# LN1 statistics by sums and squares on ScalarE, and one of GpSimd's eight heads of tile 2 on VectorE

## The chip, the cores and the metric

The kernel runs on one core of a Trainium2 chip. The metric is the device time of that core in microseconds (us), the median of three runs. The engines are called as the profile calls them: PE is TensorE (matmuls), DVE is VectorE, ACT is ScalarE, POOL is GpSimd, SP is SyncE, which only issues DMAs.

## What is computed

8192 tokens of 256 numbers each go through an attention block, an MLP and a mixture of experts, all in fp32:

```python
def _layernorm(x, axis=-1, eps=1e-05):
    return (x - x.mean(axis)) / jnp.sqrt(x.var(axis) + eps)

x = x + _L0_attn_ref(_layernorm(x), ...)     # attention over 16 heads of one token, then an MLP with gelu
x = x + _L0_ffn_ref(_layernorm(x), ...)      # 8 experts, the two best of each token, and a shared expert

def _L0_attn_ref(q_x, ...):
    xn = _ln(q_x, ln1_w, ln1_b)              # a second normalisation, on the normalised input
    q, k, v = xn @ wq + bq, xn @ wk + bk, xn @ wv + bv      # 16 heads of 16
    fq, fk = elu(q) + 1, elu(k) + 1
    kv = einsum('bhnd,bhne->bnde', fk, v)    # sums over the heads of one token
    attn = einsum('bhnd,bnde->bhne', fq, kv) / (fq . sum_h fk + 1e-06)
    x = q_x + attn @ wo + bo
    return x + gelu(_ln(x, ln2_w, ln2_b) @ fc_w + fc_b) @ proj_w + proj_b
```

Two normalisations follow each other at the input: the outer one and LN1. Both need only the mean and the variance of a token's 256 inputs, so that they are done as one scale and one shift per token. With a variance v of the input, the product of the two factors is the root of 1/((v + eps)) times 1/(v(1 + eps) + eps*eps), up to a factor that cancels; the kernel computes both roots as exp(-0.5 ln(.)).

## The kernel before

**Blocks and stages.** The tokens are cut into 16 blocks of 512, a block into four tiles of 128 tokens, one token in each partition. The first phase, some 24 of the page's 40 slices, runs a loop over blocks, in which four stages of successive blocks overlap: in the body for block c the engines do the attention core of block c, the output projection, LN2 and the MLP of block c-1 (`stage_b`), routing and the first half of the shared expert of block c-2 (`stage_c`), and the second half of it for block c-3 (`stage_d`). The second phase gathers the tokens by expert and runs 71 expert tiles. The change touches the first phase alone.

**Who does what in a block.** PE transposes and projects each tile (`project_x`, L1256), runs the output projection (L1326), the shared expert's second half (`down`, L1420), the MLP's two layers (L1343, L1369) and the shared expert's first half (`shared_up`, L1404). The sums over heads of one token's attention are no matmuls: they are elementwise products and sums on DVE and POOL. The tiles are taken in the order 3, 0, 1, 2 (`ORDER`, L62), and their place in it, u = 0 to 3, is what the code calls a tile's number from here on. POOL does the place u = 0 whole. DVE does u = 1 and u = 3 whole. The place u = 2 (`SPLIT`) is divided: `POOL_HEADS` heads of it are POOL's, the rest DVE's (`own_heads`, L878).

**POOL's order in a block** (`body`, L553): the score products of u = 0 (L502), their sums by halving (L488, L498), the shared expert's gate product (L551), the mixing products (L509) and their sums, then `heads` (L520): the same four steps for its heads of u = 2, and last the eight indirect DMAs of `scatter` (L542). `scores` of u = 0 waits for DVE's features of that place (`feat_ready`, made at L869 near the end of DVE's body of the block before), and `heads` waits for DVE's features of u = 2 (L864).

**DVE's order in a block** (`body`, L1036): for u = 1 features, products (L884) and half of the sums (L893); then `residual_1` (L941), which waits for PE's output projection (L947), adds it and takes LN2's statistics; `keep_scales` (L855); `ln1_stats` for the next block (L830); `scales_b` (L848), which waits for ACT's reciprocal root of LN2 (`ln2_std`); the other half of the sums, the mixing products (L907); `ln1_scales` (L842), which waits for ACT's root of LN1; `choose` (routing); the sums (L920); then the same for u = 2 with DVE's heads of it, with `place` and `weights` (L1023 to L1028) in between; then u = 3 whole, with `residual_2`; and last the features of the next block's u = 0 (L869).

**LN1 statistics.** DVE takes them by `bn_stats` of each tile (L820) and `bn_aggr` (L827), which leaves mean and variance in `mv_a`, a piece of a PSUM bank. Two small operations add the epsilons (L836, L837). ACT takes logarithm and exponential (`rsqrt`, L665), DVE multiplies the mean by the factors (L842: one input in PSUM, `mv_a`, the other in SBUF, `rs_a`), and ACT applies the result to `xin` later (`norm_1`, L647).

**ACT's order around the change** (`body`, L695): after the projection of u = 2 has come from PE (`take_qkv`), the root of LN2 (`rsqrt`, sq_b and rs_b), LN2's normalisation of four tiles (L644, into a piece of `hid`), then the root of LN1 (sq_a and rs_a, L722), then the two copies of the transposed LN2 output (L726, `bT`). PE's first MLP layer (L1350) waits for these copies (`hT_ready`), and ACT's gelu follows it chunk by chunk.

Every engine takes its instructions in the order in which they are written. Waits are semaphores; a wait holds everything behind it on its engine.

Of the kernel before, what the change touches and what calls it, by code (L numbers as in the profile page):

```python
# [24 lines left out]
BF16 = mybir.dt.bfloat16  # L25
# [33 lines left out]
SPLIT = 2  # L59
POOL_HEADS = 8  # L60
RANKS_AT = 5
# [5 lines left out]
def build(nc, x, wqkv, b_tok, ln1w, ln1b, ln2w, ln2b, wo, fc_w, fc_b, proj_w, gate_w, sg_up, sg_down,  # L67
          experts, out):
    ctx = ExitStack()
    with ctx:  # L70
        def sb(name, shape, dt=FP32):
            return ctx.enter_context(nc.sbuf_tensor(name, shape, dt))

        def sem(name):
            return ctx.enter_context(nc.semaphore(name))
# [58 lines left out]
        rs_c = sb("rs_c", [P, 2, TPB])  # L134
        eps_1 = sb("eps_1", [P, 1])
        neg_1 = sb("neg_1", [P, 1])
        act_tmp = sb("act_tmp", [P, 4])
# [54 lines left out]
        def small(j):  # L192
            used = [D]

            def piece(n):
                used[0] += n
                assert used[0] <= 2 * D
                return p_qk[j][:, used[0] - n:used[0]]
            return (piece(2 * TPB).rearrange("p (t s) -> p t s", s=2),
                    piece(2 * TPB).rearrange("p (t s) -> p t s", s=2),  # L200
                    piece(3 * HEADS))
        mv_a, mv_b, _ = small(1)
        den = [small(j)[2] for j in range(2)]
# [19 lines left out]
        bias_ready = sem("bias_ready")  # L223
        xin_loaded = sem("xin_loaded")
        ln1_var = sem("ln1_var")
        ln1_log = sem("ln1_log")
# [73 lines left out]
        def wait(eng, s, value):  # L300

            if not isinstance(value, int) or value > 0:
                eng.wait_ge(s, value)
# [305 lines left out]
        def _(act):  # L609
# [31 lines left out]
            def norm(dst, src, scales, ready):  # L641

                for t in range(TPB):
                    a.activation(dst(t), src(t), ACT.Identity, bias=scales[:, 1, t:t + 1],  # L644
                                 scale=scales[:, 0, t:t + 1]).then_inc(ready, 1)

            def norm_1(b):  # L647
                wait(act, ln1_scale, b + 1)
                norm(lambda t: xin[:, t, :], lambda t: xin[:, t, :], rs_a[:, 1:4:2], xhat_ready)
# [45 lines left out]
            def body(c, j):  # L695
# [24 lines left out]
                if more:  # L720
                    wait(act, ln1_var, c + 2)
                    rsqrt(rs_a[:, 0:2], sq_a[:], ln1_log, ln1_std, c + 2)  # L722
                if stage_b:
# [36 lines left out]
            table_exp_ln()  # L760
            wait(act, ln1_var, 1)
            rsqrt(rs_a[:, 0:2], sq_a[:], ln1_log, ln1_std, 1)
            norm_1(0)
# [50 lines left out]
        def _(dve):  # L814
# [14 lines left out]

            def ln1_stats(b):  # L830

                wait(dve, xin_loaded, 16 * (b + 1))
                stats(lambda t: xin[:, t, :], mv_a)
                done.later(v.tensor_scalar(sq_a[:, 0, :], mv_a[:, :, 1], 1.0, EPS, ALU.mult, ALU.add))  # L836
                v.tensor_scalar(sq_a[:, 1, :], mv_a[:, :, 1], 1.0 + EPS, EPS * EPS,  # L837
                                              ALU.mult, ALU.add).then_inc(ln1_var, 1)

            def ln1_scales(b):  # L840
                wait(dve, ln1_std, b + 1)
                v.scalar_tensor_tensor(rs_a[:, 2:4], mv_a[:, :, 0].unsqueeze(1).to_broadcast([P, 2, TPB]), -1.0,  # L842
                                       rs_a[:, 0:2], ALU.mult, ALU.mult).then_inc(ln1_scale, 1)
# [192 lines left out]
            def body(c, j):  # L1036
# [10 lines left out]
                if core:  # L1047
                    keep_scales(c)
                    if more:
                        ln1_stats(c + 1)  # L1050
                if stage_b:
# [87 lines left out]

            dve.wait_ge(pool_const, 4)  # L1140
            ln1_stats(0)
            done(v.memset(neg_1[:], -1.0))
            done(v.memset(eps_1[:], EPS))
            announce(dve, v.memset(act_tmp[:], 0.0), tmp_ready, 1)
            ln1_scales(0)


# [416 lines left out]
```

## Time and profile before

| | us |
|---|---|
| median of three runs (lowest, highest) | 1806.62 (1806.27, 1808.12) |
| the profiled execution's own time | 1806.18 |
| its span, from the first to the last instruction | 1804.5 |

| engine | busy us | share of the span |
|---|---|---|
| PE matmuls | 1700.4 | 94% |
| POOL | 1244.4 | 69% |
| DVE | 1214.8 | 67% |
| ACT | 723.5 | 40% |

The shares are averages over two very different phases. In the page's forty slices DVE and POOL stand at eight or nine tenths in the first 24 slices, which is the block loop, and at two or three tenths after that; PE stands at nine tenths in both. The mean granted PE clock of the whole span is 0.971. The chain that ended last, followed back through the whole span, is 43% PE, 41% POOL, 7% DVE and 7% issue.

How to read it: a row of the timeline begins with the start and the duration in us, then the engine, the line, the operation, what it writes and reads, and in brackets the idle time of the engine before it and what ended that. "x4" is four instructions of one kind in a row. Rows of grouped lines end with the busy time in us, the mean duration of one instruction in ns, and the idle time before.

### The profile page before, as it was taken

Reading aid. Unit: us, or ns where it says so; the run is one execution under the profiler, and the core shown is the slowest. Engines: PE = TensorE matmul, PEld = TensorE weight load, DVE = VectorE, ACT = ScalarE, POOL = GpSimd, SP = SyncE. Lnnn points to the kernel's source line nnn. Section 1 sums busy time; section 2 is a strip of 40 time slices with the busy share of each in tenths; the row PEclk is TensorE's granted clock in tenths of the full one; section 3 lists DMA queues with packets and bytes.
Section 4 is the critical chain, followed back from the end, with each engine's and each line's share of the span. In section 5 each row is a group of like instructions: output and inputs, shape, how many; then the busy total and the mean of one; then the engine's idle time right before and its main releaser. Section 6 shows DMA issues by size and latency. Waiting matters only on the chain.

```text
span 1804.5 us, 25211 instructions
## 1 busy us (share of the span) xinstructions
PE 1700.4 (94%) x7288; PEld 1236.1 (69%) x7289; DVE 1214.8 (67%) x2292; ACT 723.5 (40%) x1469; POOL 1244.4 (69%) x652
## 2 busy tenths in 40 slices
PE   2588999999999999999999998989999999999997
PEld 1354675665666666666666666658888888888886
DVE  7999999999999999999999986132222222222221
ACT  2244445445455355355354363322323232323232
POOL 5988899999999899898899994223333333333333
PEclk8688999999999999999999999989999999999999
DMA  5101101101101101101101101156777677777774
GB/s 199 43 4 59 48 21 39 60 15 44 56 15 47 47 23 47 47 23 47 47 23 47 47 13 36 36 155 162 167 154 169 151 167 155 168 152 165 156 167 78
DMA packets 87150, 148.79 MB, mean 82 GB/s; under 512 B 8640, under 2 KB 71872, under 8 KB 86720
## 3 DMA queue, kind: packets, MB, share of 16 engines
q1 hardware_dynamic: 60512, 112.58, 20.0%
q0 software_dynamic: 26592, 35.67, 12.0%
q8 instruction: 20, 0.33, 0.1%
q14 instruction: 26, 0.21, 0.0%
HBM read 101.79 MB, written 48.56 MB: 83 GB/s over the span
## 4 chain that ended last, share of the span: by engine, by line
PE 43%; POOL 41%; issue 7%; DVE 7%; DMA 1%; ACT 1%; POOLq 1%; SPq 0%; DVEq 0%; ACTq 0%
POOL prod_pool L488 16%; PE p_b L1473 10%; PE p_b L1484 10%; POOL prod_pool L509 8%; POOL prod_pool L502 7%; PE p_q L1473 7%; POOL rows_sorted L542 5%; PE p_b L1301 4%; PE p_v L1473 3%; PE p_b L1350 2%; POOL sg_g L551 2%; PE p_xT L1460 2%; PE p_b L1416 2%; DVE p_q L893 1%; DVE prod L884 1%
## 5 line engine op out<-in xcount | busy, mean ns | idle before, releaser
L596 POOL DMA_INDIRECT out_rows<-prod_pool,prod x142 | 220.7, 1554 | 384.1 <-ACT prod_pool L790 353.7
L488 POOL TENSOR_TENSOR prod_pool<-prod_pool 128x2048 f32<-128x2048 f32 (+2 forms) x192 | 400.9, 2088 | 15.1
L1350 PE MATMUL p_b<-bT,fc_sb 128*128 128x512 f32 x512 | 230.7, 605 | 1.3 <-ACT bT L726 1.3
L1301 PE MATMUL p_b<-proj_sb,hid 128*128 128x256 f32 x1024 | 231.6, 379 | 0.0
L1301 PEld LDWEIGHTS p_b<-proj_sb,hid 128*128 128x128 f32 x1024 | 189.8, 190 | 29.2 <-issue 0.5
L1473 PE MATMUL p_b<-prod,exp_up 128*128 128x256 f32 x840 | 187.1, 379 | 0.0
L1416 PE MATMUL p_b<-x3T,sgup_sb 128*128 128x512 f32 x384 | 177.3, 601 | 5.4 <-DVEq L968 3.5
L884 DVE TENSOR_TENSOR prod<-p_q,eqk 128x4096 f32<-128x4096 f32 (+1 forms) x48 | 178.3, 3714 | 4.8
L893 DVE TENSOR_REDUCE p_q<-prod 128x128 f32<-128x2048 f32 x64 | 180.7, 2823 | 1.2
L907 DVE TENSOR_TENSOR prod<-p_q,v_dve 128x4096 f32<-128x4096 f32 (+1 forms) x48 | 178.2, 3713 | 1.7
L920 DVE TENSOR_REDUCE qkv<-prod 128x256 f32<-128x4096 f32 (+1 forms) x48 | 178.0, 3709 | 1.7
L1350 PEld LDWEIGHTS p_b<-bT,fc_sb 128*128 128x128 f32 x512 | 97.6, 193 | 113.2 <-issue 106.0
L1473 PEld LDWEIGHTS p_b<-prod,exp_up 128*128 128x128 f32 x840 | 157.0, 190 | 19.8
L1235 DVE TENSOR_TENSOR prod_pool<-prod,p_b 128x256 f32<-128x256 f32 x105 | 44.2, 421 | 180.9 <-ACT prod L782 130.4
L542 POOL DMA_INDIRECT rows_sorted<-rows,slot x128 | 127.0, 992 | 51.0 <-issue 37.5
L1273 PE MATMUL p_q<-wqkv_sb,xnT 128*128 128x512 f32 x256 | 128.3, 625 | 33.0 <-DVEq L939 21.4
L502 POOL TENSOR_TENSOR prod_pool<-fqk_pool 128x4096 f32<-128x4096 f32 x16 | 121.0, 7562 | 31.4 <-DVE fqk_pool L869 30.7
L731 ACT ACTIVATE hid<-p_b,fcb_sb 128x512 f32<-128x512 f32 x128 | 87.9, 687 | 128.4 <-PE p_b L1350 128.4
L1473 PE MATMUL p_q<-prod,exp_up 128*128 128x256 f32 x576 | 132.7, 384 | 0.0
L1416 PEld LDWEIGHTS p_b<-x3T,sgup_sb 128*128 128x128 f32 x384 | 69.1, 192 | 86.4 <-issue 65.2
L629 ACT ACTIVATE eqk<-p_q,neg 128x512 f32<-128x512 f32 x64 | 44.0, 687 | 209.4 <-PE p_v L1278 160.3
L790 ACT ACTIVATE prod_pool<-p_b,prod 128x256 f32<-128x256 f32 x142 | 59.5, 470 | 160.5 <-PE p_b L1484 156.0
(175 smaller groups left out, 2965.4 us busy)
## 6 DMA issues: line engine op xcount, KB each, us to landing
exp_up<-in_experts SPq DMA_DIRECT2D x71, 768.0 KB
prod<-rows_sorted SPq DMA_DIRECT2D x71, 260.0 KB
xin<-in_x SPq DMA_DIRECT2D x16, 512.0 KB, 3.5
xres<-in_x SPq DMA_DIRECT2D x16, 512.0 KB
out_rows<-x SPq DMA_DIRECT2D x16, 512.0 KB, 2.9
exp_dn<-in_experts SPq DMA_DIRECT2D x8, 384.0 KB, 5.6
out_rows<-prod_pool,prod POOLq DMA_INDIRECT x142, 3.8
rows_sorted<-rows SPq DMA_DIRECT2D x2, 1040.0 KB, 7.1
```

What stands on the lines that cost most here:

```text
L488: done(g.tensor_tensor(prod_pool[:, at:at + n * w], prod_pool[:, at:at + n * w], prod_pool[:, at + n * w:at + 2 * n * w], ALU.add))
L502: return g.tensor_tensor(prod_pool[:, 0:n * HH].rearrange("p (d h g) -> p d h g", d=HD, g=HEADS), q.rearrange("p (h d) -> p d h", d=HD).un ...
L542: pool.indirect_dma_start(out=rows_sorted[:, :], out_offset=bass.IndirectOffsetOnAxis(ap=slot[:, s * TPB + t:s * TPB + t + 1], axis=0), in ...
L596: pool.indirect_dma_start(out=out[:, :], out_offset=bass.IndirectOffsetOnAxis(ap=tok_i[j][:, a:a + 1], axis=0), in_=yg[j][:, a * D:(a + 1) ...
L884: done.later(v.tensor_tensor(prod[:, 0:n * HH].rearrange("p (h g d) -> p h g d", h=n, g=HEADS), p_qk[u % 2][:, 0:n * HD].rearrange("p (h d ...
L893: done.later(v.tensor_reduce(p_qk[u % 2][:, lo * HEADS:hi * HEADS], prod[:, lo * HH:hi * HH].rearrange("p (a d) -> p a d", d=HD), AX.X, AL ...
L907: ins = v.tensor_tensor(prod[:, 0:n * HH].rearrange("p (h e g) -> p h e g", h=n, e=HD), p_qk[u % 2][:, 0:n * HEADS].rearrange("p (h g) -> ...
L1301: ins = t_.matmul(o, src[:, k, t * P:(t + 1) * P], w[:, k, :], start=k == 0, stop=bias_at is None and k == chunks - 1)
L1350: ins = t_.matmul(bnk[:], fc_sb[:, k, f * P:(f + 1) * P], bT[:, k, :], start=k == 0, stop=k == KC - 1)
L1416: ins = t_.matmul(bnk[:], sgup_sb[:, k, lo:lo + P], x3T[:, k, :], start=k == 0, stop=k == KC - 1)
L1473: ins = t_.matmul(gu_banks[j][i][:, part * TILE:(part + 1) * TILE], exp_up[j][:, at:at + P], xgT[j][:, c * TILE:(c + 1) * TILE], start=c = ...
L1484: ins = t_.matmul(y_bank[:, h * D:(h + 1) * D], hgT[j][:, i * TILE + h * P:i * TILE + (h + 1) * P], exp_w(e, at, at + D), start=i == 0, st ...
```

## The change

LN1's statistics move from DVE to ACT. `ln1_stats` on DVE goes: four `bn_stats`, four `bn_aggr` and two `tensor_scalar` in each block. In the place of `rsqrt` for LN1, ACT runs a new `ln1_scales`: it waits for the block's input (`xin_loaded`) and for `keep_scales`, and sums each tile by a Copy with an accumulator output, turns the four sums into means with the sign changed, sums the squares of (x - mean) by a Square with the mean as a bias and an accumulator output, and takes two logarithms with the two epsilons as biases and one exponential. It waits four times for its own results on the way. DVE's `ln1_scales` now reads the mean from `mean_a`, which lies in SBUF, where `mv_a` was in PSUM. `POOL_HEADS` falls from 8 to 7, so that DVE has 9 of the 16 heads of u = 2 in place of 8. At the start, DVE's three small memsets (now four) no longer stand behind the statistics of block 0.

```diff
-POOL_HEADS = 8
+POOL_HEADS = 7
...
+        sum_a = sb("sum_a", [P, TPB])
+        mean_a = sb("mean_a", [P, TPB])
+        square_a = sb("square_a", [P, TPB])
+        act_junk = sb("act_junk", [P, TPB, D], BF16)
...
-        mv_a, mv_b, _ = small(1)
+        _, mv_b, _ = small(1)
...
+            def ln1_scales(b):
+                wait(act, xin_loaded, 16 * (b + 1))
+                wait(act, scale_ready, b)
+                for t in range(TPB):
+                    a.activation(act_junk[:, t, :], xin[:, t, :], ACT.Copy, accum_out=sum_a[:, t:t + 1]).then_inc(ln1_sum, 1)
+                act.wait_ge(ln1_sum, TPB * (b + 1))
+                a.activation(mean_a[:], sum_a[:], ACT.Copy, scale=-1.0 / D).then_inc(ln1_mean, 1)
+                act.wait_ge(ln1_mean, b + 1)
+                for t in range(TPB):
+                    a.activation(act_junk[:, t, :], xin[:, t, :], ACT.Square, bias=mean_a[:, t:t + 1],
+                                 accum_out=square_a[:, t:t + 1]).then_inc(ln1_var, 1)
+                act.wait_ge(ln1_var, TPB * (b + 1))
+                a.activation(sq_a[:, 0, :], square_a[:], ACT.Ln, bias=eps_1[:, 0:1], scale=1.0 / D).then_inc(ln1_log, 1)
+                a.activation(sq_a[:, 1, :], square_a[:], ACT.Ln, bias=eps_2[:, 0:1], scale=(1.0 + EPS) / D
+                             ).then_inc(ln1_log, 1)
+                act.wait_ge(ln1_log, 2 * (b + 1))
+                a.activation(rs_a[:, 0:2], sq_a[:], ACT.Exp, scale=-0.5).then_inc(ln1_std, 1)
...
                 if more:
-                    wait(act, ln1_var, c + 2)
-                    rsqrt(rs_a[:, 0:2], sq_a[:], ln1_log, ln1_std, c + 2)
+                    ln1_scales(c + 1)
...
-            def ln1_stats(b):
-                wait(dve, xin_loaded, 16 * (b + 1))
-                stats(lambda t: xin[:, t, :], mv_a)
-                done.later(v.tensor_scalar(sq_a[:, 0, :], mv_a[:, :, 1], 1.0, EPS, ALU.mult, ALU.add))
-                v.tensor_scalar(sq_a[:, 1, :], mv_a[:, :, 1], 1.0 + EPS, EPS * EPS,
-                                              ALU.mult, ALU.add).then_inc(ln1_var, 1)
...
             def ln1_scales(b):
                 wait(dve, ln1_std, b + 1)
-                v.scalar_tensor_tensor(rs_a[:, 2:4], mv_a[:, :, 0].unsqueeze(1).to_broadcast([P, 2, TPB]), -1.0,
+                v.scalar_tensor_tensor(rs_a[:, 2:4], mean_a[:].unsqueeze(1).to_broadcast([P, 2, TPB]), 1.0,
                                        rs_a[:, 0:2], ALU.mult, ALU.mult).then_inc(ln1_scale, 1)
...
                     keep_scales(c)
-                    if more:
-                        ln1_stats(c + 1)
                 if stage_b:
                     scales_b(ln2_std, ln2_scale, c)
```

## Rows read from the trace of the kernel before

**Rows 1.** Timeline of POOL, block 13, and its first product in blocks 2 and 14.

```profile
140.50 7.55 POOL L502 TENSOR_TENSOR prod_pool<-fqk_pool 128x4096 f32<-128x4096 f32 x1 [9.66 <-DVE fqk_pool L869]
...
897.87 7.57 POOL L502 TENSOR_TENSOR prod_pool<-fqk_pool 128x4096 f32<-128x4096 f32 x1
918.34 7.56 POOL L509 TENSOR_TENSOR prod_pool<-s_pool,v_pool 128x4096 f32<-128x4096 f32 x1
925.98 8.31 POOL L488 TENSOR_TENSOR prod_pool<-prod_pool 128x2048 f32<-128x2048 f32 x3
935.26 4.88 POOL L502 TENSOR_TENSOR prod_pool<-eqk 128x2048 f32<-128x2048 f32 x1 [0.16 <-POOL qkv_pool L498]
945.38 4.89 POOL L509 TENSOR_TENSOR prod_pool<-s_pool,v_dve 128x2048 f32<-128x2048 f32 x1
...
966.97 7.57 POOL L502 TENSOR_TENSOR prod_pool<-fqk_pool 128x4096 f32<-128x4096 f32 x1
```

**Rows 2.** Timeline of DVE, block 13.

```profile
896.71 0.58 DVE L869 SCALAR_TENSOR_TENSOR fqk_pool<-eqk,p_q 128x256 f32<-128x256 f32 x1
...
912.38 1.29 DVE L947 TENSOR_TENSOR xmid<-xmid,p_b 128x512 f32<-128x512 f32 x2 [1.15 <-PE p_b L1306]
...
915.83 1.39 DVE L820 BATCH_NORM_STATS2 st<-xin 128x6 f32<-128x256 f32 x4
...
917.93 0.15 DVE L848 SCALAR_TENSOR_TENSOR rs_b<-p_q,rs_b 128x4 f32<-128x4 f32 x1
...
925.13 0.15 DVE L842 SCALAR_TENSOR_TENSOR rs_a<-p_q,rs_a 128x8 f32<-128x8 f32 x1
...
932.50 0.29 DVE L864 SCALAR_TENSOR_TENSOR p_q<-eqk,p_q 128x128 f32<-128x128 f32 x1
...
942.65 0.17 DVE L1028 TENSOR_TENSOR rows<-gap_e,rows 128x4 f32<-128x4 f32 x1
...
964.68 0.58 DVE L869 SCALAR_TENSOR_TENSOR fqk_pool<-eqk,p_q 128x256 f32<-128x256 f32 x1
```

**Rows 3.** Timeline of DVE in block 15, the last, which takes no LN1 statistics.

```profile
1056.68 0.16 DVE L848 SCALAR_TENSOR_TENSOR rs_b<-p_q,rs_b 128x4 f32<-128x4 f32 x1 [1.95 <-ACT rs_b L669]
```

**Rows 4.** Timeline of ACT, block 13.

```profile
917.62 0.21 ACT L669 ACTIVATE rs_b<-sq_b 128x4 f32<-128x4 f32 x1
918.12 2.08 ACT L644 ACTIVATE hid<-xmid,rs_b 128x256 f32<-128x256 f32 x4 [0.29 <-DVE rs_b L848]
920.10 0.20 ACT L667 ACTIVATE sq_a<-sq_a 128x8 f32<-128x8 f32 x1
...
923.27 1.45 ACT L726 ACTIVATE bT<-p_b,ln_sb 128x512 f32<-128x512 f32 x2 [2.73 <-PE p_b L1287]
```

**Rows 5.** Timeline of PE, block 13.

```profile
894.26 1.95 PE L1273 MATMUL p_q<-wqkv_sb,xnT 128*128 128x512 f32 x4 [0.48 <-DVE prod L907]
...
924.48 10.46 PE L1350 MATMUL p_b<-bT,fc_sb 128*128 128x512 f32 x24
...
962.60 1.88 PE L1273 MATMUL p_q<-wqkv_sb,xnT 128*128 128x512 f32 x4
```

**Rows 6.** DVE by line and shape, 275 to 1036 us (11 blocks).

```profile
L884 DVE TENSOR_TENSOR prod<-p_q,eqk 128x4096 f32<-128x4096 f32 x22 | 97.3, 4425 | 1.8
...
L884 DVE TENSOR_TENSOR prod<-p_q,eqk 128x2048 f32<-128x2048 f32 x11 | 25.2, 2292 | 1.5
```

**Rows 7.** POOL by line and shape, 275 to 1036 us (11 blocks).

```profile
L488 POOL TENSOR_TENSOR prod_pool<-prod_pool 128x1024 f32<-128x1024 f32 x44 | 103.9, 2361 | 3.5
...
L488 POOL TENSOR_TENSOR prod_pool<-prod_pool 128x512 f32<-128x512 f32 x44 | 56.0, 1273 | 3.4
```

**Rows 8.** ACT by line and shape, whole span.

```profile
L638 ACT ACTIVATE v_dve<-p_v 128x256 f32<-128x256 f32 x48 | 18.0, 375 | 0.0
```

**Rows 9.** Timeline of DVE at 597 us.

```profile
597.10 1.01 DVE L1028 TENSOR_TENSOR rows<-gap_e,rows 128x4 f32<-128x4 f32 x1
```

**Rows 10.** The chain that ended last at 597 us: start, us, what.

```profile
596.82 1.27 POOL prod_pool L488
```

More of the change, by code:

```diff
@@ L135, in build @@
         eps_1 = sb("eps_1", [P, 1])
+        eps_2 = sb("eps_2", [P, 1])
+        sum_a = sb("sum_a", [P, TPB])
+        mean_a = sb("mean_a", [P, TPB])
+        square_a = sb("square_a", [P, TPB])
+        act_junk = sb("act_junk", [P, TPB, D], BF16)
         neg_1 = sb("neg_1", [P, 1])
@@ L224, in build @@
         xin_loaded = sem("xin_loaded")
+        ln1_sum = sem("ln1_sum")
+        ln1_mean = sem("ln1_mean")
         ln1_var = sem("ln1_var")
@@ L760, in _ @@
             table_exp_ln()
-            wait(act, ln1_var, 1)
-            rsqrt(rs_a[:, 0:2], sq_a[:], ln1_log, ln1_std, 1)
+            ln1_scales(0)
             norm_1(0)
@@ L1138, in body @@
                         dve.sem_inc(pq_free, 1)
-            dve.wait_ge(pool_const, 4)
-            ln1_stats(0)
             done(v.memset(neg_1[:], -1.0))
             done(v.memset(eps_1[:], EPS))
+            done(v.memset(eps_2[:], EPS * EPS))
             announce(dve, v.memset(act_tmp[:], 0.0), tmp_ready, 1)
+            dve.wait_ge(pool_const, 4)
             ln1_scales(0)
```

## The prediction

> **What bounds the kernel now.** I read the page's slices first: only the first 24 of 40, the block loop, have DVE and POOL near full, and the change touches only that loop. There the chain of waits runs through POOL alone, so I went to POOL's timeline [rows 1]. In block 13 its work stands end to end: it begins the block at 897.87 and the next at 966.97, a period of 69.10 us, with no wait for another engine. The bound on the loop is POOL.
>
> Next comes DVE's timeline [rows 2], since DVE gets work and loses work. From the end of the features for u = 0 (896.71 + 0.58 = 897.29) to the same point a block later (965.26) is 67.97 us. POOL started 0.58 us after those features were ready, so DVE and PE are only about 1.1 us per block faster than POOL. The reader should take from this that a shorter POOL uncovers at most 1.1 us per block before another loop binds; the question is what the change does to that other loop.
>
> That loop goes through three engines. DVE waits 1.15 us for PE's output projection at L947 [rows 2]; PE in turn waited 0.48 us for DVE's mixing product before the projection of the next block's u = 1 [rows 5]; and ACT stands between them.
>
> **POOL's part.** A halving of 1024 columns takes 2361 ns, of 512 columns 1273 ns [rows 7]: 2.1 ns per column and 0.18 us fixed. With seven heads each halving loses an eighth of its columns (128, 64, 32, 16): 0.51 us for the four, twice in `heads`. Each of its two products takes 4.88 us [rows 1]; an eighth of that without the fixed part is 0.59 us, twice. Together 2.2 us, so POOL alone would need 66.9 us. Even if the products cost the same as now, it would need 68.1.
>
> **DVE's added head.** A product over 4096 elements takes 4425 ns and over 2048 2292 ns [rows 6], so 256 more elements cost 0.27 us. Two products and two sums of u = 2 grow by that: 1.08 us with the small totals. All of it lies in DVE's unbroken run between L947 and the next block's features, with nothing to hide it.
>
> **DVE's removed statistics.** From 915.83 to the start of L848 at 917.93 DVE did LN1's statistics: 2.10 us [rows 2]. It looks like a gain of 2.1. But L848 waits for ACT's root of LN2, which ended at 917.62 + 0.21 = 917.83 [rows 4], 0.10 us before DVE got there. That root follows PE's projection of u = 2 and cannot come earlier by this change. So DVE gets 0.1 us and waits for the other 2.0. The trace of before holds the case: block 15 takes no statistics for a next block, and there DVE waits 1.95 us for ACT at L848 [rows 3]. Above, the gain is bounded by the full 2.1 us. I take 0.1. DVE's loop becomes 67.97 - 0.1 + 1.08 = 68.95 us.
>
> **The moved operand.** L842 had one input in PSUM; now both, `mean_a` and `rs_a`, are in SBUF. The trace has another small DVE operation with two SBUF inputs, L1028: 0.17 us in block 13 [rows 2], but 1.01 us at 597.10 [rows 9], when POOL was in a halving from 596.82 to 598.09 [rows 10]; it ended 0.02 us after POOL's operation did. So such an operation stands until POOL's current one is over. L842 itself now takes 0.15 us in the midst of POOL's 7.56 us mixing product (918.34 to 925.90) [rows 1, 2]. What it costs depends on where it lands. If it lands in that product's tail, it waits for the end; if it comes after it, the next halving holds it for 4.5 us (8.31 us is that halving with two shorter ones). Below, zero, if only L1028's kind of operation is held.
>
> The Trainium skill ("SBUF — State Buffer", section "Who interferes with whom") says that any DVE instruction with two SBUF inputs contends with a GpSimd instruction that reads SBUF, the later one waiting out the earlier. By that L842 is held like L1028; by the rows alone a different operation need not be, and that is the no-change rival below.
>
> Positions, counted from the end of the features: POOL, no longer late, starts about 0.1 after them (ACT's row at 918.12 began 0.04 after L848, for which it waited, had ended [rows 2, 4]), so the mixing product ends at 28.1 and the halving behind it at 32.7. L842 arrives at 925.13 - 897.29 - 0.1 = 27.7: it waits 0.4 and ends at 28.2. The features of u = 2 end 7.5 later (932.50 + 0.29 - 925.28), and L1028 follows them by 9.86 + 0.82 = 10.7, at 46.4. POOL begins `heads` at 37.5 and its mixing product of them, now 10.1 - 1.1 = 9.0 later, at 46.5 [rows 1]: L1028 slips in 0.1 us ahead of it. From L1028 to the next features was 22.6 us; with the last of the four grown operations it is 22.9. The loop closes at 69.3 us, against 69.1 now. With a miss at L842 everything behind it comes 4.5 later, POOL waits for the features of u = 2, L1028 falls into POOL's product of `heads` and is held another 2.6: 69.3 + 7.1 = 76.4 us for that block.
>
> **ACT's part.** The root of LN1 began at 920.10 and the next work, the copies of bT, waited for PE until 923.27 [rows 4]. Into this go four copies, four squares, and four small operations with waits. A copy of 256 columns takes 375 ns [rows 8], four normalisations with scale and bias 2.08 us [rows 4]. Copies at the one and squares at the other price: 1.5 + 2.1; the small ones at 0.20 each and the waits at 0.04: 0.9. No row shows an accumulator output: between nothing and a small operation of 0.21 each (1.7 us); I take 0.3, since such an operation overlaps its neighbours. Sum 4.8 us, bounds 3.8 (all eight at 375 ns) and 6.2.
>
> The Trainium skill ("ScalarE: Activation LUTs", "What ACT_TABLE_LOAD costs") prices an activation at 186 ns plus 0.833 ns a column, 93 ns more for a pointer operand, with 93 ns of overlap. By that page, as an estimate, the eight take 2.8 us and the whole 4.0.
>
> The copies of bT then start at 924.9 in place of 923.27, 1.6 late; PE's first MLP layer at 924.48 stood 0.4 behind what its input needed (1.21 after the copies began, of which the first takes about 0.8), so it starts 1.2 late. PE's loop, 68.34 from 894.26 to 962.60 [rows 5], becomes 69.5, 0.2 over the loop above. PE thus falls behind by 0.2 per block, L947 and L842 come later, and once 0.5 is gone L842 misses. A miss holds DVE and lets PE catch up. I count a miss in a quarter to a third of the blocks.
>
> **The sum**, against the profiled execution's own 1806.2: twelve blocks of the steady loop (blocks 3 to 14) at +0.2, 2 us; two or three misses at 7.1, 17; and blocks 0 to 2, where POOL waits for DVE already (9.66 us in block 2, [rows 1]), so that DVE's added head and one hold of L842 count, 3. Together +22, 1828. The median of the runs stands 0.4 above the profiled one; I forecast 1828 for it too.
>
> **Rivals.**
> - Faster: POOL was the only bound, and DVE's freed time counts. It decides at L848: if ACT's root of LN2 came 1 us or more earlier, DVE would need 67.97 - 2.1 + 1.08 = 67.0, and PE's 68.3 would bind: 0.8 less in twelve blocks, 1796. For it: POOL's chain. Against it: block 15's wait.
> - No change: L842 is not held, and the statistics fit on ACT in 4 us. Then the loop is 68.95: -2 us, 1804; with blocks 0 to 2 about 1806. Against it: L1028.
> - Much slower: L842 misses in every block. It decides at 5.4 us of statistics on ACT (the root of LN1 is then ready only at 28.1), or where L1028 comes 0.1 us later than I have it, which costs 4.3 by itself. 7.3 us in twelve blocks and 3: 1897.
>
> **Chances.** Forecast 0.50, faster 0.13, no change 0.12, much slower 0.25. The forecast's own range is 1811 to 1850, from no miss to a miss in every second block. The range for 8 in 10 leaves out half of the faster rival and the dearer half of the slow one: 1801 to 1893. A change under 0.2% (3.6 us) can't be told from none: faster 0.13, the same 0.12, slower 0.75.
>
> **What would show it.** In the profile of the changed kernel: DVE idle about 2 us at L848 in each block, released by ACT; L842 no longer 0.15 us but 0.4 in the good blocks and over 4 in the others, ending with an operation of POOL; POOL idle before its first product; ACT without idle time ahead of bT, and PE idle before its first MLP layer. It is wrong if L848 shows no wait, if L842 stays at 0.15, or if POOL is still without gaps.

## The result, and the profile after

| | before | after |
|---|---|---|
| median of four runs (lowest, highest), us | 1806.44 (1806.07, 1808.12) | 1868.51 (1864.39, 1886.59) |
| the profiled execution's own time | 1806.18 | 1864.39 |
| its span | 1804.5 | 1862.3 |
| POOL busy | 1244.4 | 1209.0 |
| DVE busy | 1214.8 | 1244.8 |
| ACT busy | 723.5 | 789.0 |

The ratio is 1.0361, 95% interval 1.0293 to 1.0429: slower, by 62 us at the median. The forecast was 1828 with a range of 1801 to 1893. Of one kernel further down, the one before with seven heads on POOL, the eight runs lie between 1812.6 and 1871.7 us: its ratio counts only the three within 1.5% of the fastest, and its profile is of one that is not among them.

The line numbers shift. In the changed kernel the scale of LN2 is L862 (before: L848), the multiply of the LN1 scale L856 (L842), DVE's addition of the output projection L961 (L947), the product of the second gap weight L1042 (L1028), POOL's products L509 and L516 (L502, L509), its halvings L495 (L488).

DVE's timeline after, four rows of block 7 (its features end at 494.05) and the same four of block 12 (858.67):

```profile
509.08 1.29 DVE L961 TENSOR_TENSOR xmid<-xmid,p_b 128x512 f32<-128x512 f32 x2 [1.10 <-PE p_b L1318]
...
514.55 0.16 DVE L862 SCALAR_TENSOR_TENSOR rs_b<-p_q,rs_b 128x4 f32<-128x4 f32 x1 [1.94 <-ACT rs_b L695]
...
521.76 0.43 DVE L856 SCALAR_TENSOR_TENSOR rs_a<-mean_a,rs_a 128x8 f32<-128x8 f32 x1
...
540.38 0.17 DVE L1042 TENSOR_TENSOR rows<-gap_e,rows 128x4 f32<-128x4 f32 x1
...
875.38 1.28 DVE L961 TENSOR_TENSOR xmid<-xmid,p_b 128x512 f32<-128x512 f32 x2 [2.78 <-PE p_b L1318]
...
880.94 0.16 DVE L862 SCALAR_TENSOR_TENSOR rs_b<-p_q,rs_b 128x4 f32<-128x4 f32 x1 [2.03 <-ACT rs_b L695]
...
888.15 3.27 DVE L856 SCALAR_TENSOR_TENSOR rs_a<-mean_a,rs_a 128x8 f32<-128x8 f32 x1
...
909.61 2.69 DVE L1042 TENSOR_TENSOR rows<-gap_e,rows 128x4 f32<-128x4 f32 x1
```

POOL's timeline after, the operations beside them:

```profile
494.13 7.56 POOL L509 TENSOR_TENSOR prod_pool<-fqk_pool 128x4096 f32<-128x4096 f32 x1 [2.65 <-DVE fqk_pool L883]
...
858.76 7.55 POOL L509 TENSOR_TENSOR prod_pool<-fqk_pool 128x4096 f32<-128x4096 f32 x1 [6.64 <-DVE fqk_pool L883]
...
879.24 7.55 POOL L516 TENSOR_TENSOR prod_pool<-s_pool,v_pool 128x4096 f32<-128x4096 f32 x1
886.87 8.29 POOL L495 TENSOR_TENSOR prod_pool<-prod_pool 128x2048 f32<-128x2048 f32 x3
...
899.00 4.30 POOL L509 TENSOR_TENSOR prod_pool<-eqk 128x1792 f32<-128x1792 f32 x1 [3.03 <-DVE p_q L878]
...
907.99 4.28 POOL L516 TENSOR_TENSOR prod_pool<-s_pool,v_dve 128x1792 f32<-128x1792 f32 x1
```

Against [rows 1, 2]: POOL, which had no wait, now stands 2.65 us ahead of its first product in the good block and 6.64 in the bad one. DVE has the forecast hole of 2 us at L862 in both. In the bad block L856 takes 3.27 us, L1042 2.69, and both end with an operation of POOL: L856 at 891.41, the first of POOL's three halvings of L495 at 891.39; L1042 at 912.30, POOL's mixing product of `heads` at 912.27. The good block lasts 69.22 us, from 494.05 to 563.27; the bad one 76.35, from 858.67 to 935.02. Of the twelve blocks 3 to 14 five are good (69.13 to 69.53), two, blocks 5 and 9, have L1042 held alone (73.84 and 73.51), and the last five of them, from 706 us on, have both held (76.33 to 76.65). In block 5 L1042 starts 0.07 us behind POOL's mixing product of `heads`; DVE's row, then POOL's:

```profile
397.23 4.22 DVE L1042 TENSOR_TENSOR rows<-gap_e,rows 128x4 f32<-128x4 f32 x1
```

```profile
397.16 4.27 POOL L516 TENSOR_TENSOR prod_pool<-s_pool,v_dve 128x1792 f32<-128x1792 f32 x1
```

ACT's timeline after, LN1 in block 7 (one row of each kind) and the copies of bT behind it:

```profile
516.73 0.40 ACT L659 ACTIVATE act_junk<-xin 128x256 bf16<-128x256 f32 x1
517.03 0.19 ACT L659 ACTIVATION_READ_ACCUMULATOR act_junk<-xin 128x1 f32 x1
...
518.69 0.51 ACT L664 ACTIVATE act_junk<-xin,mean_a 128x256 bf16<-128x256 f32 x1
...
521.32 0.21 ACT L671 ACTIVATE rs_a<-sq_a 128x8 f32<-128x8 f32 x1
521.43 1.43 ACT L751 ACTIVATE bT<-p_b,ln_sb 128x512 f32<-128x512 f32 x2
```

PE's timeline after: the first MLP layer of block 7, and the projection of the next u = 1 at the end of block 5 (L1042 held), of block 7 (good) and of block 11 (both held):

```profile
421.50 1.96 PE L1285 MATMUL p_q<-wqkv_sb,xnT 128*128 128x512 f32 x4 [3.72 <-DVE prod L921]
...
522.25 10.57 PE L1362 MATMUL p_b<-bT,fc_sb 128*128 128x512 f32 x24 [1.21 <-ACT bT L751]
...
560.48 1.88 PE L1285 MATMUL p_q<-wqkv_sb,xnT 128*128 128x512 f32 x4
...
855.65 3.01 PE L1285 MATMUL p_q<-wqkv_sb,xnT 128*128 128x512 f32 x4 [3.97 <-DVE prod L921]
```

The windows of the trace after (stretch, length, busy time of PE, PEld, DVE, ACT, POOL, then the granted clock, DMA share, GB/s): a good block, a bad one, and 3.4 us behind two of PE's waits, the one ahead of block 6 (from its end on) and the one ahead of block 12 (from 0.8 us after its end on):

```profile
563.00:632.00 69.00, 67.10 (x275) 43.49 (x276) 63.52 (x91) 37.97 (x83) 61.73 (x31) 1.00 0.11 38
859.00:935.00 76.00, 69.38 (x275) 44.43 (x277) 69.17 (x90) 37.95 (x83) 61.49 (x31) 0.97 0.10 35
421.50:424.92 3.42, 3.42 (x12) 1.91 (x13) 2.83 (x11) 0.24 (x1) 0.31 (x1) 1.00 0.08 10
856.41:859.83 3.42, 3.42 (x7) 1.79 (x6) 2.87 (x10) 0.00 (x0) 1.07 (x1) 0.50 0.21 55
```

In a good block PE has no wait before that projection, against 0.48 us in [rows 5]. Behind a held L1042 it waits 3.4 to 4.4 us for DVE's mixing product, from block 5 on. Behind block 5 that had no consequence: the granted clock stayed at 1.00, the four matmuls took 1.96 us, and block 6 was good. From block 9 on the granted clock fell to 0.50 (the 1.2 GHz level) in each of these places, the matmuls took 3.01 us and more in place of 1.88, and every following block was held.

### The profile page after: what moved, and what is told of

The parts are those of the page before. It is cut to its first block, busy times and chain, and to the rows that moved or that the text cites. A ratio compares the mean times of both kernels' runs of the same rounds, so it can differ in the third digit from the quotient of the medians.

```text
span 1862.3 us, 25313 instructions
## 1 busy us (share of the span) xinstructions
PE 1704.2 (92%) x7243; PEld 1232.9 (66%) x7289; DVE 1244.8 (67%) x2133; ACT 789.0 (42%) x1757; POOL 1209.0 (65%) x652
## 4 chain that ended last, share of the span: by engine, by line
PE 59%; DVE 25%; ACT 7%; issue 5%; DMA 1%; POOL 1%; SPq 0%; ACTq 0%; POOLq 0%; DVEq 0%
PE p_b L1485 10%; PE p_b L1496 10%; PE p_q L1485 7%; PE p_b L1428 7%; PE p_b L1313 6%; DVE prod L921 6%; PE p_b L1362 5%; DVE p_q L907 5%; PE p_q L1285 4%; DVE prod L898 4%; PE p_v L1485 3%; PE p_v L1285 2%; DVE qkv L934 2%; PE p_xT L1472 2%; DVE rows L1042 2%
## 5 line engine op out<-in xcount | busy, mean ns | idle before, releaser
L495 POOL TENSOR_TENSOR prod_pool<-prod_pool 128x2048 f32<-128x2048 f32 (+2 forms) x192 | 385.4, 2007 | 15.1
L1285 PE MATMUL p_q<-wqkv_sb,xnT 128*128 128x512 f32 x256 | 137.1, 663 | 59.6 <-DVE prod L921 39.9
L898 DVE TENSOR_TENSOR prod<-p_q,eqk 128x4096 f32<-128x4096 f32 (+1 forms) x48 | 182.5, 3802 | 5.5 <-DVE attn L947 1.1
L509 POOL TENSOR_TENSOR prod_pool<-fqk_pool 128x4096 f32<-128x4096 f32 x16 | 120.9, 7555 | 100.2 <-DVE fqk_pool L883 100.2
L907 DVE TENSOR_REDUCE p_q<-prod 128x128 f32<-128x2048 f32 (+1 forms) x64 | 185.0, 2891 | 1.2
L921 DVE TENSOR_TENSOR prod<-p_q,v_dve 128x4096 f32<-128x4096 f32 (+1 forms) x48 | 182.5, 3802 | 1.7
L934 DVE TENSOR_REDUCE qkv<-prod 128x256 f32<-128x4096 f32 (+1 forms) x48 | 182.3, 3798 | 1.6
```

The lines of the kernel that those rows point to most:

```text
L495: done(g.tensor_tensor(prod_pool[:, at:at + n * w], prod_pool[:, at:at + n * w], prod_pool[:, at + n * w:at + 2 * n * w], ALU.add))
L898: done.later(v.tensor_tensor(prod[:, 0:n * HH].rearrange("p (h g d) -> p h g d", h=n, g=HEADS), p_qk[u % 2][:, 0:n * HD].rearrange("p (h d ...
L907: done.later(v.tensor_reduce(p_qk[u % 2][:, lo * HEADS:hi * HEADS], prod[:, lo * HH:hi * HH].rearrange("p (a d) -> p a d", d=HD), AX.X, AL ...
L921: ins = v.tensor_tensor(prod[:, 0:n * HH].rearrange("p (h e g) -> p h e g", h=n, e=HD), p_qk[u % 2][:, 0:n * HEADS].rearrange("p (h g) -> ...
L934: done.later(v.tensor_reduce(qkv[u % 2][:, 0:n].rearrange("p h e -> p (h e)"), prod[:, 0:n * HH].rearrange("p (a g) -> p a g", g=HEADS), A ...
L1285: t_.matmul(bnk[:, 0:hi - lo], xnT[u % 2][:, k, :], wqkv_sb[:, k, lo:hi], start=k == 0, stop=False)
```

## The experiments

The theory at first was: L856 and L1042, each with two SBUF inputs, stand until POOL's operation ends, L856 before all; a block in which they do is late, and TensorE's half clock keeps the next one late. The rivals: (A) LN1's 4.8 us on ACT ahead of bT by themselves, (B) DVE's added head by itself. Every run has its own comparison with the kernel before, whose median was 1805.67, 1806.83 and 1806.05 in the three sets. The table gives, from each profiled execution, the place of DVE's rows for the features of u = 0 at the start of block 3 and the mean of the twelve blocks from there to block 15.

| kernel | median us | ratio, 95% | block 3 begins | mean block |
|---|---|---|---|---|
| before | 1806.4 | 1 | 206.00 | 69.11 |
| after | 1868.5 | 1.0361 (1.0293 to 1.0429) | 212.30 | 73.00 |
| mean from PSUM | 1856.6 | 1.0277 (1.0255 to 1.0299) | 210.49 | 72.52 |
| weight with one SBUF input | 1872.7 | 1.0383 (1.0323 to 1.0443) | 212.88 | 73.46 |
| both of these | 1854.1 | 1.0264 (1.0247 to 1.0282) | 211.60 | 72.52 |
| weights from PSUM | 1823.9 | 1.0096 (1.0079 to 1.0113) | 208.94 | 70.12 |
| both from PSUM | 1815.1 | 1.0049 (1.0033 to 1.0065) | 210.45 | 69.53 |
| eight heads on POOL | 1826.3 | 1.0107 (1.0091 to 1.0123) | 208.71 | 70.96 |
| before, seven heads | 1844.7 | 1.0071 (1.0035 to 1.0107) | 210.88 | 72.21 |
| before, seven heads, weights from PSUM | 1810.7 | 1.0025 (1.0015 to 1.0034) | 206.71 | 69.18 |
| before, mean in SBUF | 1818.4 | 1.0061 (1.0044 to 1.0078) | 220.71 | 69.10 |
| both from PSUM, hole filled | 1812.9 | 1.0040 (1.0025 to 1.0054) | 209.82 | 69.50 |
| both from PSUM, LN1 split | 1811.1 | 1.0028 (1.0016 to 1.0040) | 205.63 | 69.48 |
| both from PSUM, split and filled | 1793.6 | 0.9929 (0.9915 to 0.9943) | 210.59 | 67.96 |

### The mean from PSUM

```
-  v.scalar_tensor_tensor(rs_a[:, 2:4], mean_a[:]..., 1.0, rs_a[:, 0:2], ALU.mult, ALU.mult)
+  done(v.tensor_copy(mean_p, mean_a[:]))          # mean_p: where mv_a was, in PSUM
+  v.scalar_tensor_tensor(rs_a[:, 2:4], mean_p...,  1.0, rs_a[:, 0:2], ALU.mult, ALU.mult)
```

> The changed kernel, but VectorE first copies the mean to PSUM (one input, 128x4) and the multiply of the LN1 scale reads it there, as the kernel does in LN3: one SBUF input instead of two. Theory (the multiply with two SBUF inputs stands until GpSimd's operation ends): the multiply takes 0.2 us in every block, the blocks of 76.4 us are gone; the multiply of the gap weights still has two SBUF inputs and comes 0.2 us ahead of GpSimd's mixing product, so some blocks of 73.5 stay; 1806 to 1830 us. Rival A (the 4.8 us of LN1 on ScalarE ahead of bT are the cause, the held operation only shows it): no change, 1860 to 1870. Rival B (the added head on VectorE is the cause): the same 1860 to 1870.

1856.6 us: a gain of 12 where the theory wanted 38 or more. DVE's timeline, block 9 and the start of the next:

```profile
672.08 0.17 DVE L858 SCALAR_TENSOR_TENSOR rs_a<-p_q,rs_a 128x8 f32<-128x8 f32 x1
...
690.48 4.19 DVE L1044 TENSOR_TENSOR rows<-gap_e,rows 128x4 f32<-128x4 f32 x1
...
734.09 1.29 DVE L963 TENSOR_TENSOR xmid<-xmid,p_b 128x512 f32<-128x512 f32 x2 [2.78 <-PE p_b L1320]
```

PE's timeline between them, and the window of the first 3 us of that projection:

```profile
714.36 3.65 PE L1287 MATMUL p_q<-wqkv_sb,xnT 128*128 128x512 f32 x4 [3.58 <-DVE prod L923]
```

```profile
714.36:717.37 3.01, 3.01 (x4) 1.45 (x5) 2.61 (x9) 0.00 (x0) 0.00 (x0) 0.50 0.00 0
```

The LN1 multiply takes 0.17 us in every block, so its hold is gone. The weights' multiply, 0.1 us behind the start of POOL's mixing product of `heads`, is held 4.19 us by itself; PE then waits 3.58 us, projects in 3.65 us instead of 1.88, and the next output projection comes 1.6 us late (2.78 against 1.1 to 1.3). That is enough for the next block to be held too: nine of the twelve take 73.28 us or more. A late block makes the next one late without a held LN1 multiply. What differs from the changed kernel is that here it ends with the second block: that one is held 2.7 us only, PE then waits 2.1 us (behind blocks 4, 7, 10 and 12) in place of 4.0, the clock stays at 1.00 and the output projection is in time. The next miss still comes soon, as L1044 stands within 0.1 us of the start of POOL's product even in a good block.

### The second weight with one SBUF input, alone and with the mean from PSUM

```
-  v.tensor_tensor(rows[..., C_W1], gap_e[:], rows[..., C_W0], ALU.mult)
+  v.tensor_scalar(rows[..., C_W1], rows[..., C_W0], -1.0, 1.0, ALU.mult, ALU.add)
```

> The changed kernel, but the second gap weight is 1 minus the first (one SBUF input) instead of the product of two SBUF operands. Theory: this operation takes 0.2 us everywhere; in the changed kernel it was the first to be held (blocks 5 and 9) before the LN1 multiply was; without it the LN1 multiply has to slip by itself past the end of GpSimd's mixing product, for which it has 0.1 to 0.4 us: 1806 to 1820 us if it never does after the start, 1860 if it does once and for good. Rival A and B: 1860 to 1870.

> Both of these edits on the changed kernel, nothing else: LN1 on ScalarE and seven heads stay. Theory: no VectorE operation of either line is held, all blocks take 69.1 to 69.5 us, 1803 to 1809 us, no slower than before the change. Rival A (LN1 on ScalarE ahead of bT) and rival B (the added head): 1840 to 1870 as TensorE's or VectorE's loop stays too long.

1872.7 and 1854.1 us: neither did anything beside what the mean did. The timelines of the second in block 6, DVE first, then POOL:

```profile
474.21 4.16 DVE L1044 TENSOR_SCALAR rows<-rows 128x4 f32<-128x4 f32 x1
```

```profile
474.07 4.27 POOL L517 TENSOR_TENSOR prod_pool<-s_pool,v_dve 128x1792 f32<-128x1792 f32 x1
```

One SBUF input is not enough: this operation too ends 0.03 us after POOL's (478.37, 478.34). What it shares with the held ones is that nothing of it lies in PSUM. That alone does not make an operation wait: the TENSOR_REDUCE of `keep_scales` (L869 of the changed kernel, 8 elements, from SBUF to SBUF) takes 0.16 us each of the fifteen times that it runs in the midst of an operation of POOL. The Trainium skill ("SBUF — State Buffer", section "Who interferes with whom") has both cases: a copy, cast or tensor_scalar can enter a mode that uses the port pair shared with GpSimd, and an operation with two SBUF inputs reads through it. These rows agree, with 4.16 us.

### Both from PSUM

```
+  done(v.reciprocal(gap_1, gap_1))                           # gap_1 is in PSUM
+  done.later(v.tensor_copy(rows[..., C_W0], gap_1))
+  v.tensor_tensor(rows[..., C_W1], gap_e[:], gap_1, ALU.mult)
```

> The run before this showed that a multiply-and-add of one SBUF operand that also writes SBUF is held like one with two SBUF inputs (4.16 us in block 6 of that run), so the gap weights were not freed. Here the reciprocal goes to PSUM and both weights are made from there; the mean is read from PSUM too. LN1 on ScalarE and seven heads stay. Theory: with neither operation held, all blocks take 69.2 to 69.6 us and nothing is late later: 1806 to 1815 us. Rival A (the 4.8 us of LN1 on ScalarE ahead of bT set the loop): 1840 or more with no operation held. Rival B (VectorE's added head): 1830 or more.

1815.1 us, at the upper end of what was expected. DVE's timeline in block 6:

```profile
440.40 0.16 DVE L864 SCALAR_TENSOR_TENSOR rs_b<-p_q,rs_b 128x4 f32<-128x4 f32 x1 [2.03 <-ACT rs_b L696]
...
447.79 0.17 DVE L858 SCALAR_TENSOR_TENSOR rs_a<-p_q,rs_a 128x8 f32<-128x8 f32 x1
...
466.27 0.15 DVE L1045 TENSOR_TENSOR rows<-gap_e,p_q 128x4 f32<-128x4 f32 x1
```

Neither is held in any block. 53 of the 62 us are gone while LN1 stays on ACT and the head on DVE, so rivals A and B hold for the other 8 at most. The blocks take 69.53 us, 0.4 more than before: the sum of the forecast had 0.2. Of what is left, 5.0 us are these twelve blocks and 4.4 the later start of block 3.

### The weights from PSUM alone

> The changed kernel with the gap weights made from PSUM alone; the LN1 multiply keeps its two SBUF inputs. Theory: the weights take 0.15 us everywhere, the LN1 multiply is still held up to 4.5 us where it comes after the end of GpSimd's mixing product, and TensorE does not catch up behind such a block: 1830 to 1860 us. If a held LN1 multiply were harmless by itself: 1811 to 1817, as with both freed.

1823.9 us, between the two expectations. DVE's timeline, blocks 10 and 11:

```profile
727.45 4.51 DVE L856 SCALAR_TENSOR_TENSOR rs_a<-mean_a,rs_a 128x8 f32<-128x8 f32 x1
...
750.23 0.15 DVE L1043 TENSOR_TENSOR rows<-gap_e,p_q 128x4 f32<-128x4 f32 x1
...
788.19 1.28 DVE L961 TENSOR_TENSOR xmid<-xmid,p_b 128x512 f32<-128x512 f32 x2 [1.17 <-PE p_b L1319]
...
800.87 0.36 DVE L856 SCALAR_TENSOR_TENSOR rs_a<-mean_a,rs_a 128x8 f32<-128x8 f32 x1
```

A block with L856 held lasts 73.85 to 73.94 us, and the next is good: L961 waits 1.17 again, L856 0.36. It happens in two of the twelve blocks. A held LN1 multiply by itself does let PE catch up; the theory that no miss does falls. With the runs above this splits the 62 us: the weights' multiply 44.6 (1868.5 - 1823.9), the LN1 multiply 8.8 (1823.9 - 1815.1), all else 8.3 (1815.1 - 1806.8). Freed in the other order, the LN1 multiply brings 11.9 (1868.5 - 1856.6) and the weights' 41.5 (1856.6 - 1815.1).

### Each half of the change by itself

The changed kernel with `POOL_HEADS = 8`, and the kernel before with `POOL_HEADS = 7`:

> The changed kernel with eight heads on GpSimd again: LN1 on ScalarE alone, both operations with all operands in SBUF as in the changed kernel. Theory: GpSimd's 69.1 us bound the block, VectorE has 1 us to spare and comes back after a held operation; 1806 to 1835 us. Rival A (LN1 on ScalarE): 1855 to 1870, as the changed kernel. Rival B (the added head): 1800 to 1808.

> The kernel before with seven of GpSimd's heads and nothing else: LN1 stays on VectorE with its mean in PSUM. Theory: VectorE's own work 69.0 to 69.2 us a block, the LN1 multiply is never held, the gap weights' multiply may be (4 us in some blocks): 1803 to 1825 us. Rival B (the added head alone makes VectorE too slow): over 1840. Rival A says nothing of it but 1800 to 1810.

With eight heads 1826.3 us: L856 is held 3.6 to 4.4 us in every second block (4.37 us at 804.92, 0.37 at 877.11), each time the next block is good, and L1042 stays under 0.7 us from block 4 on. The blocks take 72.7 to 73.7 and 68.6 to 68.9 us in turn, at a granted clock of 1.00. LN1 on ACT, with its mean in SBUF, costs 19.5 us by itself here.

With seven heads alone the eight runs lie between 1812.6 and 1871.7 us. The profiled one is of 1848. L842 is never held (0.15 us), its mean being in PSUM; L1028 is, 2.7 to 3.8 us, in each block from 2 to 10, and then the blocks turn good (69.0 to 69.3). DVE's timeline in the last held block, 10, and the first good one, 11:

```profile
744.06 1.28 DVE L947 TENSOR_TENSOR xmid<-xmid,p_b 128x512 f32<-128x512 f32 x2 [2.73 <-PE p_b L1306]
...
775.16 3.01 DVE L1028 TENSOR_TENSOR rows<-gap_e,rows 128x4 f32<-128x4 f32 x1
...
815.99 1.28 DVE L947 TENSOR_TENSOR xmid<-xmid,p_b 128x512 f32<-128x512 f32 x2 [1.17 <-PE p_b L1306]
...
847.09 0.22 DVE L1028 TENSOR_TENSOR rows<-gap_e,rows 128x4 f32<-128x4 f32 x1
```

PE's timeline ahead of each of the two, and the windows of 3 us from these places on:

```profile
724.39 3.59 PE L1273 MATMUL p_q<-wqkv_sb,xnT 128*128 128x512 f32 x4 [3.40 <-DVE prod L907]
...
797.87 1.95 PE L1273 MATMUL p_q<-wqkv_sb,xnT 128*128 128x512 f32 x4 [3.71 <-DVE prod L907]
```

```profile
724.39:727.40 3.01, 3.01 (x4) 1.45 (x5) 2.61 (x9) 0.00 (x0) 0.00 (x0) 0.50 0.00 0
797.87:800.88 3.01, 3.01 (x11) 1.74 (x12) 2.61 (x9) 0.00 (x0) 0.00 (x0) 1.00 0.00 0
```

This is the clearest comparison of the study. PE has waited 3.4 to 4.0 us for DVE behind each of the nine held blocks. Behind the first eight the clock fell to 0.50, the output projection came late (DVE waited 2.6 to 4.1 us for it, 2.73 in block 10) and the next block was held; behind the ninth, with as long a wait (3.71), it stayed at 1.00, the output projection came in time (1.17), and the chain was over. How soon such a chain ends would be why the runs differ by 59 us; that was seen in one profile only. The expectation (to 1825) was too low for six of the eight runs. The same kernel with the weights from PSUM:

> The kernel before with seven heads on GpSimd and the gap weights made from PSUM (LN1 on VectorE, its mean in PSUM as before). Theory: the times of 1812 to 1872 of the seven heads alone were the weights' multiply, held 2.7 to 4 us; with it freed no block is over 69.6 us and the time is 1804 to 1812, with little spread. Rival (the added head itself): 1830 or more.

1810.7 us, 1806.5 to 1811.9 over ten runs, the largest block of the twelve 69.37. The head itself costs 0.25% (0.15 to 0.34); what it did was to move L1028 onto POOL's product.

### The mean in SBUF, alone

```
-  mv_a, mv_b, _ = small(1)                  # PSUM
+  _, mv_b, _ = small(1)
+  mv_a = sb("mv_a", [P, TPB, 2])
```

> The kernel before with the LN1 mean and variance kept in SBUF instead of PSUM, nothing else: LN1 on VectorE, eight heads on GpSimd. Theory: the multiply of the LN1 scale now has two SBUF inputs and stands till GpSimd's mixing product ends (about 0.8 us), or 4.5 us where it comes just after that; with VectorE's 1.1 us to spare 1806 to 1820 us. If the placement of the mean mattered only with LN1 on ScalarE: 1804 to 1808.

1818.4 us, as expected in size, but only in the smaller part from the multiply. DVE's timeline in blocks 2 and 13:

```profile
168.21 5.28 DVE L837 TENSOR_SCALAR sq_a<-mv_a 128x4 f32<-128x4 f32 x1
...
932.33 0.52 DVE L837 TENSOR_SCALAR sq_a<-mv_a 128x4 f32<-128x4 f32 x1
...
940.02 0.47 DVE L843 SCALAR_TENSOR_TENSOR rs_a<-mv_a,rs_a 128x8 f32<-128x8 f32 x1
```

In the steady blocks each of them is held 0.3 to 0.4 us, DVE has that to spare, and the block takes 69.10. The loss is made before block 3, which begins 14.7 us later: in blocks 0, 1 and 2 the epsilon's operation L837, now from SBUF to SBUF, is held 2.1, 5.2 and 5.1 us, the multiply 2.4, 1.1 and 1.1. The edit moved the operands of the epsilons' operations too, and so doesn't price the multiply alone; it shows that the place where such an operation lands sets its price.

### A version that beats both

On top of both operands from PSUM, two edits, each also alone:

```
 # split: ACT takes two squares behind the first gelus, and the roots behind the last
-  ln1_scales(c + 1)
+  ln1_sums(c + 1); ln1_squares(c + 1, range(2))
...
+      if f < 2: ln1_squares(c + 1, range(f + 2, f + 3))      # behind gelu f
   table_exp_ln()
+  ln1_roots(c + 1)
 # DVE: ln1_scales(c + 1) goes behind products_2(c, 2)
 # fill: DVE's second part of the sums of u = 1 ahead of the LN2 scale
-  sums_1(1, 0, half)     ...   scales_b(...); sums_1(1, half, HEADS)
+  sums_1(1, 0, half + 1) ...   sums_1(1, half + 1, HEADS); scales_b(...)
```

> A version meant to beat both kernels: both operations from PSUM as above; of LN1 on ScalarE only the four sums and two squares stay ahead of bT, the other two squares go behind the first two gelus and the roots behind the last; VectorE makes its LN1 scale after the second mixing product of tile 2; and VectorE's second half of the score sums (7 of 16 heads) goes ahead of the LN2 scale, into the 2 us in which it waits for ScalarE's root. Theory: TensorE's 1.2 us wait for bT and VectorE's 2 us hole go, the block falls to 68.0 to 68.5 us (TensorE's own loop of 67.7 and its latencies): 1788 to 1798 us. Rival: the block stays at 69.1 to 69.3 as something else closes the loop: 1803 to 1810.

> The same without the filled hole. Theory: VectorE's loop of 69.1 to 69.3 with its hole of 2 us remains, TensorE's wait is gone: 1800 to 1808 us. Rival (TensorE's wait was what closed the loop): the same time as with the hole filled, 1788 to 1798.

> The version with both operations from PSUM (LN1 whole ahead of bT on ScalarE, seven heads), and VectorE's 2 us hole filled with the second half of the score sums. Theory: TensorE waits for bT as before, and its loop of fc to the output projection and VectorE's and ScalarE's chain from there back to bT adds up to 69.2 to 69.4 us whether VectorE has work in the hole or not: 1808 to 1816 us, no better than without it, and only with the split of LN1 does filling pay. Rival (the hole alone is what binds): 1793 to 1800.

Together 1793.6 us, 13 less than before the change and 75 less than after it. DVE's timeline of block 11, features to features:

```profile
753.78 0.58 DVE L896 SCALAR_TENSOR_TENSOR fqk_pool<-eqk,p_q 128x256 f32<-128x256 f32 x1
...
769.64 1.28 DVE L974 TENSOR_TENSOR xmid<-xmid,p_b 128x512 f32<-128x512 f32 x2 [1.10 <-PE p_b L1333]
...
775.26 0.15 DVE L875 SCALAR_TENSOR_TENSOR rs_b<-p_q,rs_b 128x4 f32<-128x4 f32 x1
...
821.75 0.58 DVE L896 SCALAR_TENSOR_TENSOR fqk_pool<-eqk,p_q 128x256 f32<-128x256 f32 x1
```

PE's first MLP layer in it, without a wait:

```profile
781.44 10.46 PE L1377 MATMUL p_b<-bT,fc_sb 128*128 128x512 f32 x24
```

The hole at L875 is gone, PE's 1.2 us wait for bT too, and the block takes 67.97 us, 1.1 under the old bound of POOL. Alone, neither edit shortens the block: split only, DVE still waits 1.7 to 2.0 us for the root of LN2 (1.71 at 781.93; the block takes 69.48 us); filled only, PE still waits 1.21 us at 794.70 for bT (69.50). Two loops of nearly one length stood side by side, DVE's and PE's, and each edit takes one of them away. The 1811.1 of the split alone is over its expectation (to 1808): its blocks take 69.48 us where 69.1 to 69.3 had been expected.

## Why the prediction was right, and where not

- **POOL's part, right.** Its products with seven heads take 4.30 and 4.28 us, as 4.88 less 0.59 said, and it is no longer the bound: it waits 2.65 us in a good block.
- **The removed statistics, right.** L862 waits 1.6 to 2.1 us for ACT's root of LN2 in every block from 3 on, and the 2.1 us of statistics bring nothing; the filled-hole runs show that this time is worth something only if PE is freed as well.
- **The added head, right.** The good blocks take 69.13 to 69.53 us; forecast 69.3. With the statistics left on DVE, seven heads and the weights from PSUM the shortest block takes 69.05, which is 67.97 + 1.08.
- **ACT's part, right in its sum, by luck in its terms.** From 883.12 to 887.92 in block 12 it takes 4.80 us, as forecast. The accumulator reads, of which no row told, cost 0.09 to 0.10 each, 0.7 for the eight in place of 0.3; the copies and squares without them come to about 3.1, an estimate from their rows at the overlap of the normalisations, in place of 3.6. (The lower bound, 3.0 + 0.9, is 3.9 and not 3.8.) PE's first layer waits 1.2 us, as forecast.
- **The moved operand, right in its mechanism and its positions.** L856 takes 0.16 to 0.43 us in the good blocks. Where it starts behind the mixing product it stands till the halving ends, 32.7 us behind the features as forecast: 2.3 to 3.5 us in the changed kernel, as it comes there late by itself, and 4.51 with the weights from PSUM; "over 4" is not seen in the changed kernel. A block with both held takes 76.35, forecast 76.4. L1042 stood 46.36 us behind the features in block 4, forecast 46.4, 0.1 ahead of POOL's product. The drift was right too: L961 starts 15.02, 15.25 and 15.53 us behind the features in blocks 3 to 5, and L856 goes from 27.69 to 28.21, the 0.5 after which it was to miss.
- **Failed: "A miss holds DVE and lets PE catch up. I count a miss in a quarter to a third of the blocks."** It holds for a held LN1 multiply alone. It fails for the weights' multiply, which comes late in the block: from block 5 on PE waits 3.4 to 4.4 us for DVE behind it and is granted half its clock then in six of seven places, and in these six the next output projection is added 16.4 to 17.8 us behind the features in place of 15.0 to 15.5, so that the next block misses as well. (Behind block 2, where both are held too, PE waits 2.73 us, the clock stays at 1.00 and block 3 is good.) From block 9 on the changed kernel, as profiled, never leaves this. Seven of twelve blocks were held: 36.8 us for the five with both and 9.1 for the two with L1042 alone, against 17 in the sum. That PE's half clock closes the circle is read from waits of one length with and without it (behind blocks 5 and 9 of the changed kernel; ahead of blocks 10 and 11 with seven heads alone), and its size fits: 3.65 - 1.88 = 1.8 us lost, 1.6 us later. No run sets the clock by itself, and what decides whether it falls stays open.
- **Mis-sized:** blocks 0 to 2, 6.3 us for 3 (block 3 begins at 212.30 for 206.00; in block 2 both operations are held, 3.17 and 3.82 us, and not the LN1 multiply alone); the last block and what follows it, 4.8, which had no term. With 0.8 for the good blocks the terms make 6.3 + 0.8 + 9.1 + 36.8 + 4.8 = 57.8, the difference of the spans.
- **The weight of the two operations was the wrong way round.** The forecast's misses start at L842 and take L1028 along. In the steady loop L1042 was held first (block 5), and freeing it is worth 44.6 us, the LN1 multiply 8.8. The prediction had the price of L1028 by itself (4.3; the two blocks with L1042 held alone are 4.2 and 4.6 us longer than the good ones) and its margin of 0.1 us, but as the point from which the much slower rival decides, and not as the likely course. That rival came nearer than the forecast's own misses, with five blocks of its kind out of twelve. Which of the two misses first is a matter of hundredths: in blocks 5 and 9 L856 starts 0.02 us behind POOL's halving (378.89 and 378.87 in block 5) and still takes 0.16; in the kernel with the second weight from one SBUF input it starts 0.02 us behind it in block 5 (379.48 and 379.46) and is held 4.51.
- **Luck.** The time is inside the stated range of 1801 to 1893 only because that was drawn around the much slower rival too. It is outside the forecast's own 1811 to 1850, and the loss of 62 us is nearly three times the 22 of the sum. How large the loss came out owes much to where the chain starts, block 9 in the profiled run, which no run explains.

## What to carry to other kernels

A small VectorE operation with two inputs in SBUF, or a TENSOR_SCALAR from SBUF to SBUF, waited here for the end of GpSimd's current operation, up to 5.2 us, and its price was set by where it landed: list these operations, their places and GpSimd's boundaries before anything is moved, and give each one operand in PSUM. A margin of 0.1 us ahead of a 4 us hold, in a loop whose good blocks vary by 0.4 us, is not a margin. Where two engines' loops are of nearly one length, as here, an edit that frees one of them can show nothing; free both before it is judged.

## What the runs showed of the hardware

- A TENSOR_SCALAR of 4 elements a partition with its single input and its output in SBUF was held by GpSimd as long as an operation with two SBUF inputs: 4.16 us, and 5.28 us in the kernel with the mean in SBUF. A COPY of 4 elements from SBUF to PSUM (0.15 to 0.17 us) never was, nor was a TENSOR_REDUCE of 8 elements from SBUF to SBUF (0.16 us, fifteen times in the midst of an operation of GpSimd).
- A wait of TensorE of nearly one length was followed by either level of its clock: after 3.40 us by 0.50 (1.2 GHz), after 3.71 by 1.00 (2.4 GHz), in one profile.
- Each sum taken by an activation brings an instruction of its own, ACTIVATION_READ_ACCUMULATOR, of 0.19 us, of which 0.09 to 0.10 shows: normalisations of 0.59 us, without it, follow each other in 0.49, so that 0.10 is hidden; copies of 0.40 us with it follow each other in 0.40, squares of 0.49 in 0.49.
